# A gated state-space layer on one core: products of the carried state and the decayed C spread over four quarters of the TensorE array

## What is computed

```python
xn = layernorm(u)
s  = attn(xn)                    # the recurrent layer below
g  = silu(fake_quant_fp8(xn) @ fake_quant_fp8(ffn_w).T + ffn_b)
out = u + s * g
```

```python
Bx = outer(x_t, B_t)
h  = alpha_t * h + gamma_t * Bx + beta_t * previous_Bx
y  = h @ C_t                     # and y + x * D, times silu(z),
                                 # an rms norm over 2,048, an output projection
```

## Time and profile before

| | |
|---|---|
| three executions | 1485.37, 1486.18 (median), 1486.22 us |
| the profiled execution's own time | 1485.21 us |
| its span in the profile | 1483.5 us |
| busy, share of the span | PE 85%, VectorE 89%, ScalarE 53%, GpSimd 48% |
| instructions in the profile | PE 12,252, VectorE 2,280, ScalarE 1,181, GpSimd 553 |

### The profile page before, as it was taken

The page is one execution under the profiler, slowest core; times in us unless marked ns, Lnnn a source line. Parts: engine busy times, 40 slices in busy tenths (PEclk is TensorE's granted clock), DMA queues, the critical chain, the costliest instruction groups (busy, mean ns, idle before and its releaser), DMA issues. The chain is left out here.

```text
span 1483.5 us, 32371 instructions
## 1 busy us (share of the span) xinstructions
PE 1266.9 (85%) x12252; PEld 922.5 (62%) x12252; DVE 1324.3 (89%) x2280; ACT 790.1 (53%) x1181; POOL 709.0 (48%) x553
## 2 busy tenths in 40 slices
PE   2663599999999999999999999999999999999930
PEld 2552366676666666666666666667676666667620
DVE  7886599998999899989998999899998999899878
ACT  2230366656555556656655555566656556556431
POOL 6000255554555455555555555545555555455514
PEclk9855699999999999999999999999999999999965
DMA  5311442223222332234222422242223222222123
GB/s 162 114 57 39 85 100 58 58 58 73 64 54 61 87 72 58 61 68 91 51 52 46 101 57 58 61 101 58 58 60 74 65 50 61 58 58 58 30 78 92
DMA packets 63447, 101.95 MB, mean 69 GB/s; under 512 B 13547, under 2 KB 27228, under 8 KB 63068
## 3 DMA queue, kind: packets, MB, share of 16 engines
q1 hardware_dynamic: 63292, 99.88, 29.1%
HBM read 23.55 MB, written 9.18 MB: 22 GB/s over the span
## 5 line engine op out<-in xcount | busy, mean ns | idle before, releaser
L1090 POOL TENSOR_TENSOR rot<-part 128x512 f32<-128x512 f32 x256 | 354.5, 1385 | 557.6 <-DVE part L921 535.6
L921 DVE SCALAR_TENSOR_TENSOR part<-bcs,k_prmT,trig 128x512 f32<-128x512 f32 x512 | 453.1, 925 | 0.6 <-DMA trig<-tri 0.4
L939 DVE TENSOR_TENSOR M<-s,E 128x512 f32<-128x512 f32 x256 | 175.6, 686 | 66.1 <-ACT E L1039 63.3
L1039 ACT ACTIVATE E<-d 128x512 f32<-128x512 f32 x256 | 152.9, 597 | 148.5 <-PE d L745 147.8
L1120 POOL TENSOR_TENSOR sqa<-sqa,sq 128x512 f32<-128x512 f32 x112 | 142.1, 1268 | 134.2 <-ACT sq L1044 134.2
L1065 ACT ACTIVATE th<-r 128x512 f32<-128x512 f32 x128 | 76.4, 597 | 209.3 <-PE r L844 209.3
L729 PE MATMUL r<-k_w_zx,xns 128*128 128x256 f32 x512 | 139.0, 394 | 53.4 <-DVE k_carry L958 50.1
L1099 POOL TENSOR_TENSOR ce<-rot,eb 128x512 f32<-128x512 f32 x128 | 159.9, 1271 | 4.2 <-ACT eb L1061 4.2
L763 PEld LDWEIGHTS s<-rot 64*128 64x128 f32 x2048 | 125.1, 188 | 54.9 <-issue 54.1
L763 PE MATMUL s<-rot 64*128 64x128 f32 x2048 | 149.7, 286 | 0.0
L729 PEld LDWEIGHTS r<-k_w_zx,xns 128*128 128x128 f32 x512 | 93.5, 192 | 89.9 <-DVE k_carry L958 68.1
(11 more groups left out here) (233 smaller groups left out, 2096.4 us busy)
## 6 DMA issues: line engine op xcount, KB each, us to landing
trig<-tri SPq DMA_DIRECT2D x512, 128.0 KB, 2.4
bcs<-bc_t SPq DMA_DIRECT2D x16, 256.0 KB, 4.1
bcs<-bc_t SPq DMA_DIRECT2D x32, 128.0 KB, 4.0
a_big<-in_L_attn_u SPq DMA_DIRECT2D x4, 512.0 KB, 6.2
xn_t<-a_xnT SPq DMA_DIRECT2D x1, 2048.0 KB, 7.6
tc_t<-a_tcT SPq DMA_DIRECT2D x1, 2048.0 KB, 12.4
bc_t<-a_tmp SPq DMA_DIRECT2D x1, 2048.0 KB, 7.4
tcs<-tc_t SPq DMA_DIRECT2D x8, 256.0 KB, 3.2
```

The lines of the kernel that those rows point to most:

```text
L921: nc.vector.scalar_tensor_tensor(out=part[:, 2 * w + f, :], in0=bcs[:, (t + q // NQ) % 2, 2 * w + f, :], scalar=col, in1=trig[:, p, 1 - f, ...
L939: nc.vector.tensor_tensor(M[:, h, :], Sp[h % 2][:], E[:, h % 2, :], ALU.mult).then_inc(m_ready, 1)
L1039: nc.scalar.activation(E[:, h % 2, :], Dp[:], ACT.Exp).then_inc(e_ready, 1)
L1090: nc.gpsimd.tensor_tensor(rot[:, q % 2, p, w, :], part[:, 2 * w, :], part[:, 2 * w + 1, :], ALU.add).then_inc(rot_ready, 1)
```

## The change

Four things are changed.

1. In the loop PE no longer issues the products of L863 pair by pair. Both pairs get their transposes and scores-times-x products first; then 16 products of state and decayed C follow, chunk by chunk, and within a chunk in turn for (pair 0, head 0), (pair 0, head 1), (pair 1, head 0), (pair 1, head 1). The wait for the decayed C moves from the front of each pair to the front of these 16. `y_ready` is told for both pairs in the last chunk.
2. So that the four products of a chunk lie on four different quarters of the array, the two heads of the second pair change places in the output (`place`): head 0 of pair 1 is written to rows 64 to 127 of its bank, head 1 to rows 0 to 63. Which partition of the state and of C a head uses stays as it was.
3. All that carries x, z, their factors and the output weights follows that order: the load of the z and x weights is split in three DMAs, the load of `norm_w` in three, the odd blocks of the output weights are turned by two products with the identity instead of one transpose, and `kk` and `cc` are written in three pieces (`PLACES`) where there was one. A new buffer `gam` takes what `kk` held before its last step.
4. The counts of the waits for these loads are raised to match.

```diff
+PLACES = ((slice(0, 2), slice(0, 2)), (slice(2, 3), slice(3, 4)), (slice(3, 4), slice(2, 3)))
...
+        gam = sb("a_gam", [P, NC * H])
...
-            sp.dma_start(zx_nat, w_in[0:2 * DI].rearrange("(a p) m -> p a m", p=P)).then_inc(zx_loaded, 16)
+            zx = w_in[0:2 * DI].rearrange("(e b p) m -> b p e m", b=2, p=P)
+            sp.dma_start(zx_nat[:, 0:NC:2, :], zx[0]).then_inc(zx_loaded, 16)
+            for j in range(2):
+                sp.dma_start(zx_nat[64 * j:64 * j + 64, 1:NC:2, :], zx[1, 64 * (1 - j):64 * (2 - j)]).then_inc(zx_loaded, 16)
...
-            sp.dma_start(prm[0:16, :], norm_w.rearrange("(a p) -> a p", p=P)).then_inc(prm_loaded, 16)
+            nw = norm_w.rearrange("(e b p) -> b e p", b=2, p=P)
+            sp.dma_start(prm[0:16:2, :], nw[0]).then_inc(prm_loaded, 16)
+            for j in range(2):
+                sp.dma_start(prm[1:16:2, 64 * j:64 * j + 64], nw[1, :, 64 * (1 - j):64 * (2 - j)]).then_inc(prm_loaded, 16)
...
-                    last = nc.tensor.transpose(ps[g % 4][:, i * P:i * P + r], src, ident[0:r, 0:r])
+                    if 11 <= g < 15 and i % 2 == 1:
+                        for j in range(2):
+                            last = nc.tensor.matmul(ps[g % 4][64 * j:64 * j + 64, i * P:i * P + P],
+                                                    src[:, 64 * (1 - j):64 * (2 - j)], ident[:], start=True, stop=True)
+                    else:
+                        last = nc.tensor.transpose(ps[g % 4][:, i * P:i * P + r], src, ident[0:r, 0:r])
...
-            link(nc.vector.tensor_tensor(K["kk"][:], s[3][:], s[0][:], ALU.mult))
+            link(nc.vector.tensor_tensor(gam[:], s[3][:], s[0][:], ALU.mult))
...
-                link(nc.vector.tensor_tensor(K["kk"][:, a:b], K["kk"][:, a:b], ps[i][:], ALU.add))
+                by4 = lambda x: x.rearrange("p (g k) -> p g k", k=4)
+                for dst, head in PLACES:
+                    link(nc.vector.tensor_tensor(by4(K["kk"][:, a:b])[:, :, dst], by4(gam[:, a:b])[:, :, head],
+                                                 by4(ps[i][:])[:, :, head], ALU.add))
...
-            link(nc.vector.tensor_tensor(cc3, one_h(2), v3[3], ALU.subtract))
+            for dst, head in PLACES:
+                link(nc.vector.tensor_tensor(cc3[:, :, :, dst], bcast(skip[:, :, :, head], list(s3v[:, :, :, head].shape)),
+                                             s3v[:, :, :, head], ALU.subtract))
...
+        def place(p, j):
+
+            return j if p == 0 else 1 - j
...
-                                                        xk[:, par, c, (2 * p + j) * 64:(2 * p + j) * 64 + 64],
+                                                        xk[:, par, c, (2 * p + place(p, j)) * 64:(2 * p + place(p, j)) * 64 + 64],
...
                     for p in range(2):
                         pe.wait_ge(m_ready, at(T4, t, 4 * q + 2 * p + 2))
-                        pe.wait_ge(ce_ready, at(T2, t, 2 * q + p + 1))
                         pe.wait_ge(yt_ready, at(T2, t, 2 * q - 1 + p))
...
-                                nc.tensor.matmul(Yp[p][64 * j:64 * j + 64, k],
-                                                 xk[:, par, c, (2 * p + j) * 64:(2 * p + j) * 64 + 64], M[:, 2 * p + j, k],
+                                m = 64 * place(p, j)
+                                nc.tensor.matmul(Yp[p][m:m + 64, k], xk[:, par, c, 128 * p + m:128 * p + m + 64], M[:, 2 * p + j, k],
                                                  start=False, stop=False, skip_group_check=True)
-                        for c in range(CS):
-                            k = slice(c * P, c * P + P)
+
+                    pe.wait_ge(ce_ready, at(T2, t, 2 * q + 2))
+                    for c in range(CS):
+                        k = slice(c * P, c * P + P)
+                        for p in range(2):
                             for j in range(2):
                                 rows = slice(64 * j, 64 * j + 64)
-                                last = nc.tensor.matmul(Yp[p][rows, k], hs[rows, c, p, :], ce[rows, p, k],
+                                m = 64 * place(p, j)
+                                last = nc.tensor.matmul(Yp[p][m:m + 64, k], hs[rows, c, p, :], ce[rows, p, k],
                                                         start=False, stop=True, skip_group_check=True)
-                        last.then_inc(y_ready, 1)
+                            if c == CS - 1:
+                                last.then_inc(y_ready, 1)
```

More of the change, by code:

```diff
@@ L233, in _ @@
             pe.wait_ge(ident_ready, 1)
-            pe.wait_ge(zx_loaded, 16)
+            pe.wait_ge(zx_loaded, 48)
             for g, srcs in enumerate(groups):
@@ L237, in _ @@
                     pe.wait_ge(rest_loaded, 80)
-                    pe.wait_ge(prm_loaded, 16 * 17)
+                    pe.wait_ge(prm_loaded, 16 * 19)
                 if g == 11:
@@ L513, in _ @@
                 a, b = 512 * i, 512 * i + 512
-                link(nc.vector.tensor_tensor(K["kk"][:, a:b], K["kk"][:, a:b], ps[i][:], ALU.add))
+                by4 = lambda x: x.rearrange("p (g k) -> p g k", k=4)
+                for dst, head in PLACES:
+                    link(nc.vector.tensor_tensor(by4(K["kk"][:, a:b])[:, :, dst], by4(gam[:, a:b])[:, :, head],
+                                                 by4(ps[i][:])[:, :, head], ALU.add))
                 link(nc.vector.tensor_tensor(s[3][:, a:b], s[3][:, a:b], ps[i][:], ALU.mult))
-            cc3 = K["cc"][:].rearrange("p (c h) -> p c h", h=H)
-            link(nc.vector.tensor_tensor(cc3, one_h(2), v3[3], ALU.subtract))
+            cc3 = K["cc"][:].rearrange("p (c g k) -> p c g k", g=NQ, k=4)
+            s3v = s[3][:].rearrange("p (c g k) -> p c g k", g=NQ, k=4)
+            skip = rowb[:, 2 * H:3 * H].rearrange("p (g k) -> p g k", k=4).unsqueeze(1)
+            for dst, head in PLACES:
+                link(nc.vector.tensor_tensor(cc3[:, :, :, dst], bcast(skip[:, :, :, head], list(s3v[:, :, :, head].shape)),
+                                             s3v[:, :, :, head], ALU.subtract))
             for g in range(4):
```

## The result

The changed kernel took 1491.05 us (median of 10 runs, 1489.78 to 1492.77), the kernel before 1486.26 us in the same session (10 runs, 1485.03 to 1487.97). The ratio is 1.0032, with a 95% interval of 1.0023 to 1.0042: slower by 0.3%. The span of the profiled execution is 1488.1 us, where it was 1483.5.

A forecast was written before the change was run, and what follows sets the result against it. The loop of VectorE (M1 to yT0) and ScalarE (yT0 to M1) was taken to set the pace. Terms 1.9 + 1.1 + 0 to 0.5, say 3.1 us, over the median 1486.18 gave 1489.3 us, range 1485.5 to 1500.

The forecast's parts named there:

- The ring sets the pace, not PE: Loop: VectorE from M1 to yT0, then ScalarE from yT0 to M1, sets the pace; PE's y section is off it.
- The y section is 1.02 us shorter: PE in the loop: on four quarters 16 products take what 8 took, so the section is 1.02 us shorter.
- yT0 keeps its start with 0.09 us to spare: VectorE in the loop: y is ready at 872.47, yT of pair 0 starts at 872.56 as before.
- What is late next: Loop: M1 still waits for E1 and the table load; PE's 1.02 us become a wait at L743; gain nothing.
- The rule on row tiles and one bank: Skill page: different row tiles cannot access one PSUM bank simultaneously, so at most two products would overlap with the change.
- Turning the output weights, +1.9: Preparation on PE: a transpose and a pair take about 0.56 to 0.61 us, making VectorE's normalisation 1.9 us later.
- kk and cc, +1.1: Preparation on VectorE: three instructions split in three add 6 x 0.19 = 1.1 us, bounds 0.5 and 2.
- The loads, nothing: Preparation on SP's queue: the extra DMAs cost nothing, covered by PE's 9.21 us wait; otherwise about 0.5 each.
- The loop, 0 to 0.5: Loop: no gain, and a cost of 0 to 0.5 us if PE starts records more slowly in 8 first quads.
- Quads 19.1 apart (1225 / 64): Loop: sign expected in the profile after, quads on average 19.1 us apart as now.
- yT1's wait would be won: Faster rival: the 0.25 us wait comes back in each of 64 quads, about 1473 us; one in twenty.
- PE sets the pace: Faster rival: PE paces the loop, 65 us less there, about 1424 us with preparation; three in a hundred.

The follow-up runs named there:

- e1: The changed kernel with only PE's order of the products put back to pair by pair; 1491.97 us, ratio 1.0033.
- e9: The changed kernel with ScalarE's next decays ahead of each square and GpSimd's second sum of squares put off; 1467.09 us, ratio 0.987.
- e10: The kernel before with ScalarE's next decays ahead of each square and GpSimd's second sum of squares put off; 1489.68 us, ratio 1.0024.
- e7: The kernel before with only the odd blocks of the output weights turned by two products instead of a transpose; 1487.61 us, ratio 1.0008.
- e8: The kernel before with only kk and cc written in three pieces each, heads in their old places; 1489.74 us, ratio 1.0016.
- e3: The changed kernel with ScalarE taking the next quad's decays ahead of the squares; 1521.28 us, ratio 1.0234.
- e5: The changed kernel with ScalarE's decays ahead of squares and the carried-state product as a tensor_tensor; 1524.93 us, ratio 1.026.

## Why the prediction was right

The forecast was 1489.3 us, the sign a toss between "same" and "slower"; it came to 1491.05, slower. Step by step:

- *The ring sets the pace, not PE.* Right, and shown twice: PE's order put back changes nothing (e1), and cutting ScalarE's part of the ring by 0.53 us moves the step by 0.54 once nothing else eats it (e9). But PE was close behind: its own path to M1 is only 0.08 us shorter in the kernel before (e10), which the prediction did not see.
- *The y section is 1.02 us shorter.* Right: 32 records in 1.10 us. PE's busy time in the loop's stretch fell by 71.9 us.
- *yT0 keeps its start with 0.09 us to spare.* Right: in one quad the last product of y ends at 778.81 (777.71 + 1.10) and yT0 starts 0.20 us later, straight behind th; before, yT1, which waits for y, starts 0.11 us after the last product (873.38 to 873.49). The difference is the margin, 0.09.
- *What is late next.* Incomplete. I had PE wait 1 us at the exponents; it waits 0.48 us there and 0.48 us earlier, at the transposes of B (L759), for GpSimd's last rotation sum, which no step of mine named. It costs nothing, since `bw` stands behind both yT.
- *The rule on row tiles and one bank.* The sentence of the Trainium skill, "TensorEngine Tiling (Array Packing)", Restrictions and Gotchas, would have given 1.9 us or more for the 16 products. The trace has 1.10; for disjoint partitions the rule does not hold here.
- *Turning the output weights, +1.9.* Somewhat small: +2.36 from the turning's own start to the reciprocal, in e7 as in the change, with 0.63 us for a transpose and a pair where I had 0.56 to 0.61. (VectorE's second half of the scaling waits for the fourth group, whose eight pairs the sum rightly counts, and not for the third.) In the profile after only 1.26 show at the reciprocal, since the turning began at 35.71 instead of 36.80: the granted clock rises to its higher level (2.4 GHz) at 34.5 us, where the first record at that level in the trace before stands at 36.7, and the eight transposes just before the turning take 1.04 us instead of 1.74.
- *kk and cc, +1.1.* Mis-sized: +1.93, alone +1.94. I gave each extra piece a fixed 0.19 us. For `cc` it is 2.00 against 1.22 for the same 1,024 elements, 0.39 for each of two cuts, and `kk` gives 0.58 for two. A piece costs 0.3 to 0.4 us and not 0.19; this was inside the bounds of 0.5 to 2, and its 0.8 us are half of what the sum missed.
- *The loads, nothing.* Right: PE's wait before its second batch fell from 9.21 to 6.73 us, with the start 0.18 earlier.
- *The loop, 0 to 0.5.* In accord: +0.41 in 62 steps, but three traces with one and the same loop (before, e7, e8) spread from 1203.98 to 1205.13 us, so nothing can be told from that. The two terms of the preparation, 2.36 and 1.93 us, and this one make 4.7 of the 4.8 us; my sum had 1.9, 1.1 and 0 to 0.5.
- *"Quads 19.1 apart (1225 / 64)".* The number was badly formed, as the window does not hold 64 quads; the mean over 62 steps is 19.43 us, before and after.
- *The rivals.* That yT1's wait would be won: no, it turned into a longer wait before M. That PE sets the pace: no.

## What to carry to other kernels

Before shortening a busy engine's work, follow one cycle of waits around; if the engine isn't on it, the gain is nothing and the price of the new layout is all that remains. But keep the change in view: it may be the one that makes another worth having, as here, where cutting the ring pays only if PE comes to the next exponents early. The second longest path around the cycle says how much a cut can win; here it was 0.08 us behind. And when a step that should shorten the cycle makes it longer, compare the durations inside each group of instructions, since a stall beside another engine's instruction counts as work.

## What the hardware did that I had not expected

- A VectorE product of 128 x 128 from SBUF to SBUF takes 0.28 us, but 1.30 (tensor_scalar) or 1.37 us (tensor_tensor) when it starts just behind the start of a GpSimd sum of 1.27 us, in 63 quads out of 64 (e3, e5). In the changed kernel the two miss each other by a hair: the sum runs 880.92 to 882.18, and the product starts at 882.34. The rotation products do meet GpSimd's sums in the kernel before, once in nearly every quad, and take 1.75 us instead of 0.75 there.
- Four quarters of the array, with two banks of PSUM written by two heads each, run at the spacing of one: 32 records in 1.10 us for 16 float32 products of 64 x 64 by 128.
- Cutting a VectorE instruction into strided pieces of one head costs 0.3 to 0.4 us a cut.
